# Post-layernorm transformer layer on eight Trainium2 cores: bf16 operands for the layernorm sums, and two barriers replaced by single waits

## What is computed

```python
x = L0_attn_hidden_states                      # (2, 4096, 2048) f32
x = _layernorm(x + _L0_attn_ref(x, Wq, Wk, Wv, Wo), axis=-1)
x = _layernorm(x + _L0_ffn_ref(x, gate_w, gate_scale, up_w, up_scale, down_w, down_scale), axis=-1)

def _layernorm(x, axis=-1, eps=1e-5):
    m = jnp.mean(x, axis=axis, keepdims=True)
    v = jnp.var(x, axis=axis, keepdims=True)
    return (x - m) / jnp.sqrt(v + eps)
```

## Time and profile before

| what | us |
|---|---|
| runs shown: median (lowest to highest of 3) | 2450.72 (2443.09 to 2474.64) |
| the profiled execution's own time | 2434.97 |
| its span, slowest core (core 4) | 2433.4 |
| spans of the eight cores | 2421.8 to 2433.4 |
| mean granted PE clock of the cores | 0.919 to 0.924 |
| PE busy | 2058.5 (85% of the span) |
| DVE, ACT, POOL busy | 470.6, 337.3, 129.0 |

### The profile page before, as it was taken

The page is one execution under the profiler, slowest core; times in us unless marked ns, Lnnn a source line. Parts: engine busy times, 40 slices in busy tenths (PEclk is TensorE's granted clock), DMA queues, the critical chain, the costliest instruction groups (busy, mean ns, idle before and its releaser), DMA issues.

```text
span 2433.4 us, 24054 instructions; the slowest of 8 cores (2421.8 to 2433.4 us)
## 1 busy us (share of the span) xinstructions
PE 2058.5 (85%) x9445; PEld 920.9 (38%) x9624; DVE 470.6 (19%) x800; ACT 337.3 (14%) x606; POOL 129.0 (5%) x248
## 2 busy tenths in 40 slices
PE   0799766666997299999999999999999999999970
PEld 0344344444431044444443444444444443444310
DVE  0111166664111501011010000010100100000015
ACT  0000066654003310101100000011010110000030
POOL 4000000000000000000000000000000000000000
PEclk9999866666998599999999999999999999999985
DMA  9443300000420253434433333344343431333003
GB/s 221 60 75 65 69 1 1 1 1 1 78 44 0 37 102 71 86 69 80 77 69 52 69 67 58 67 78 79 70 86 70 79 60 35 59 63 69 18 0 138
DMA packets 38420, 147.70 MB, mean 61 GB/s; under 512 B 4643, under 2 KB 8869, under 8 KB 33958
## 3 DMA queue, kind: packets, MB, share of 16 engines
q0 software_dynamic: 35136, 127.94, 29.9%
q1 hardware_dynamic: 3174, 18.20, 2.3%
HBM read 265.66 MB, written 8.39 MB: 113 GB/s over the span
## 4 chain that ended last, share of the span: by engine, by line
PE 81%; DVE 7%; issue 4%; another core or an unknown queue 3%; ACT 2%; DMA 1%; DVEq 0%; ACTq 0%; POOL 0%; POOLq 0%
PE psD L769 18%; PE psG L659 18%; PE psU L667 18%; PE psW L451 5%; PE psQ L218 5%; PE psD L765 3%; PE pT L339 3%; PE psS L511 2%; PE psS L485 2%; PE pv L352 2%; DVE S_sb L574 1%; DVE S_sb L579 1%; PE psQ L227 1%; PE psH L725 1%
## 5 line engine op out<-in xcount | busy, mean ns | idle before, releaser
L659 PE MATMUL psG<-ab 128*128 128x512 bf16 x2006 | 450.8, 380 | 50.8 <-DMA ab<-wu_is 46.7
L769 PE MATMUL psD<-ab 128*128 128x512 bf16 x2004 | 448.3, 380 | 4.8 <-issue 3.7
L667 PE MATMUL psU<-ab 128*128 128x512 bf16 x2008 | 450.0, 379 | 2.1
L659 PEld LDWEIGHTS psG<-ab 128*128 128x128 bf16 x2048 | 200.7, 98 | 292.4 <-issue 52.2
L769 PEld LDWEIGHTS psD<-ab 128*128 128x128 bf16 x2048 | 195.5, 98 | 276.4 <-issue 50.8
L667 PEld LDWEIGHTS psU<-ab 128*128 128x128 bf16 x2048 | 200.3, 98 | 241.7
L679 DVE SCALAR_TENSOR_TENSOR ab<-psU,scl_sb,sq_sb 128x512 bf16<-128x512 f32 x128 | 90.2, 747 | 808.9 <-PE psU L667 794.2
L694 ACT ACTIVATE sq_sb<-psG,scl_sb 128x512 f32<-128x512 f32 x128 | 88.0, 687 | 774.3 <-PE psG L659 774.3
L339 PE MATMUL pT<-Dm_sb,ab 128*128 128x128 bf16 x640 | 75.8, 269 | 100.4 <-DVE Dm_sb L380 60.7
L779 DVE SCALAR_TENSOR_TENSOR S_sb<-psD,scl_sb,S_sb 128x1024 f32<-128x1024 f32 x32 | 41.1, 1284 | 479.8 <-PE psD L769 479.8
L218 PE MATMUL psQ<-ab 128*128 128x512 bf16 x501 | 112.0, 383 | 9.1 <-DMA ab<-wq_os 8.3
(11 more groups left out here) (72 smaller groups left out, 962.2 us busy)
## 6 DMA issues: line engine op xcount, KB each, us to landing
ab<-wg_is POOLq DMA_DIRECT2D x64, 512.0 KB, 6.0
ab<-wu_is POOLq DMA_DIRECT2D x64, 512.0 KB, 7.8
ab<-wd_os POOLq DMA_DIRECT2D x32, 1024.0 KB, 8.0
ab<-wq_os POOLq DMA_DIRECT2D x16, 512.0 KB, 5.0
ab<-wo_os POOLq DMA_DIRECT2D x16, 512.0 KB, 5.0
y<-S_sb SPq DMA_DIRECT2D x16, 512.0 KB, 7.2
ab<-x_all POOLq DMA_DIRECT2D x16, 256.0 KB, 44.3
ab<-wv_ks POOLq DMA_DIRECT2D x16, 128.0 KB, 31.3
```

The source lines that it names most:

```text
L659: last = t.matmul(psG[i % 2][:, 512 * tt:512 * tt + 512], abv(wgu_o + 4096 * (i % 2) + 128 * k, 128), abv(y1_o + 1024 * k + 512 * tt, 512) ...
L667: last = t.matmul(psU[i % 2][:, 512 * tt:512 * tt + 512], abv(wgu_o + 4096 * (i % 2) + 2048 + 128 * k, 128), abv(y1_o + 1024 * k + 512 * t ...
L769: last = t.matmul(psD[o % 2][:, 512 * tt:512 * tt + 512], abv(wd_o + 4096 * (o % 2) + 128 * i, 128), abv(h_o + 1024 * i + 512 * tt, 512), ...
```

## The change

Three edits, all in the function that builds the program:

1. The two barriers around attention are gone (they stay only in a debugging branch). In their place stand single waits: PE waits for DVE's last K cast (vv) before the scores, and for DVE and ACT (vv, ss) before the Wo projection. SP's load of the masks waits for the last V matmul (tm) and its own first loads (sq).
2. In `emit_ln` ACT first casts all 16 blocks of S_sb to bf16 into ab (at y1_o in the first layernorm, at h_o in the second). PE sums these with the bf16 ones, oncb_sb; each of its first 16 matmuls waits for its block's cast.
3. The squares are written as bf16 into two 512-wide slots of ab behind that copy, and PE sums them with oncb_sb.

The diff, cut to what is spoken of:

```diff
-            barrier()
+                barrier()
+
+            p1_vv = cnt["vv"]
+            p1_tm = cnt["tm"]
+            vt_last = max(vt_mm)
...
         @block.sync
         def _(sy):
+            sy.wait_ge(sq, p0_sq)
+            sy.wait_ge(tm, vt_last)
             inc(sy.dma_start(abv(mask_o, 8 * 640), masks[:, :]), "sq", 16)
...
             @block.tensor
             def _(t):
+                t.wait_ge(vv, p1_vv)
                 for n in range(NIT + 3):
...
-            barrier()
+                barrier()
+
+            p2_vv = cnt["vv"]
+            p2_ss = cnt["ss"]
...
+                @block.tensor
+                def _(t):
+                    t.wait_ge(vv, p2_vv)
+                    t.wait_ge(ss, p2_ss)
+
...
+                ss0_rc = cnt["ss"]
+                c_rc = [ss0_rc + k + 1 for k in range(KC)]
+
+                @block.scalar
+                def _(s):
+                    for k in range(KC):
+                        got = inc(s.copy(abv(rbf_o + 1024 * k, 1024),
+                                         S_sb[:, 1024 * k:1024 * k + 1024]), "ss")
+                        assert got == c_rc[k]
+
...
-                            last = t.matmul(psS1[:1, 512 * tt:512 * tt + 512], onc_sb[:, :1],
-                                            S_sb[:, 1024 * k + 512 * tt:1024 * k + 512 * tt + 512],
+                            if tt == 0:
+                                t.wait_ge(ss, c_rc[k])
+                            last = t.matmul(psS1[:1, 512 * tt:512 * tt + 512], oncb_sb[:, :1],
+                                            abv(rbf_o + 1024 * k + 512 * tt, 512),
...
-                            s.activation(sq_sb[:, 512 * (j % 2):512 * (j % 2) + 512],
+                            s.activation(abv(rbf_o + 16384 + 512 * (j % 2), 512),
...
-                        got = t.matmul(psS2[:1, 512 * tt:512 * tt + 512], onc_sb[:, :1],
-                                       sq_sb[:, 512 * (j % 2):512 * (j % 2) + 512],
+                        got = t.matmul(psS2[:1, 512 * tt:512 * tt + 512], oncb_sb[:, :1],
+                                       abv(rbf_o + 16384 + 512 * (j % 2), 512),
...
-        emit_ln(write_bf16_to=y1_o)
+        emit_ln(write_bf16_to=y1_o, rbf_o=y1_o)
...
-        ln2_done = emit_ln(write_bf16_to=None)
+        ln2_done = emit_ln(write_bf16_to=None, rbf_o=h_o)
```

More of the change, by code:

```diff
@@ L470, in build_nc, with emit_ln @@
         _ln_id = [0]
-        def emit_ln(write_bf16_to=None):
+        def emit_ln(write_bf16_to=None, rbf_o=None):
             _ln_id[0] += 1
```

## The result

The changed kernel took 2410.15 us (median of 9 runs, 2406.02 to 2416.31), the kernel before 2448.2 us (10 runs). The ratio is 0.9874 with a 95% interval of 0.9852 to 0.9895: 1.3% faster, some 31 us. The forecast was 2420.5 us, with 2402 to 2437 as its range, and 1.2%. The ratio leaves out runs in which the cores of one die had a lower granted clock, the median of before doesn't, so it is not the quotient of the medians. The profiled execution took 2406.02 us around a span of 2404.5; its slowest core is core 2, while in before it was core 4. Worked out from the profiled execution of before (2434.97 us), the forecast was 2404.8.

What follows compares the result with a forecast made beforehand. PE was taken to bound the kernel (81% of the wait chain), with savings only in layernorm statistics and at attention's start. Layernorms 25 plus masks 5.2 made 30.2 us off the 2450.72 us median: 2420.5 us, range 2402 to 2437.

Steps and rivals of the forecast that it cites:

- What bounds: Whole kernel: PE is 81% of the wait chain; savings possible only in the two layernorms' statistics and at attention's start.
- Casts and their table load: Start of each layernorm: 16 ACT casts at 0.95 us pace behind a table load, ending 16.6 us after ACT's release.
- PE's second half: Layernorm, after the last cast: PE's gapless matmuls for the sum's second half take 5.5 us (7.3 lower clock, 3.7 upper).
- The loop: Layernorm squares between ACT and PE: 0.625 us a square at upper clock, 0.75 at lower, 0.71 with a third upper.
- The sum per layernorm: ACT's release to DVE's first statistics step: 47.7 us (51.6 to 41.9) against 60.2; 12.5 gained each, 25 for two.
- The masks: Attention's start: earlier masks' load saves 8.3 us of DVE's wait, delays wq 0 by 3.1, net 5.2 us.
- Barriers: Around attention: replacing barriers by waits gains nothing priced above zero, at most 1.12 us; a loss is excluded.
- (a): Rival, chance 0.17: clock stays up through the layernorm statistics; two layernorms gain 36.6, in all 41.8, 2409 us.
- (b): Rival, chance 0.15: clock stays down in the layernorm statistics; 17.2 + 5.2 = 22.4 us gained, 2428 us.
- (c): Rival, chance 0.08: masks stand fully in wq 0's way before the Q projection, 9.2 us late; 24.1 gained, 2426.6 us.
- (d): Rival, chance 0.07: masks' wait at attention's start stays because something else on DVE or ACT is late; 21.9 gained, 2428.8 us.
- (e): Rival, chance 0.03: square loop loses its overlap, each square costing 1.50 us; slower by 15.6 us, 2466 us.

Runs made afterwards that it cites:

- e6: Changed kernel with four slots for the squares instead of two: 39.0 to 41.7 us per layernorm, whole kernel median 2412.4 us of 4 runs.
- e1: Changed kernel with both barriers and the old place of the masks' load back, so the layernorm part alone: ratio 0.9892 to the kernel before.
- e2: Kernel before, old layernorm, with single waits in place of the barriers and the masks loaded early: ratio 0.9992 (0.998 to 1.0003).
- e9: Changed kernel with casts on DVE, squares 1024 wide in three slots, PE summing blocks as they come, masks loaded after the fourth Q tile: 2354.96 us, ratio 0.9647.
- e3: Kernel before with only the barriers replaced by single waits, the masks' load still going out after DVE's last K cast: ratio 1.0022.
- e10: Kernel before, old layernorm, with barriers replaced by waits and the masks' load issued after the fourth Q tile: ratio 0.9991 (0.9976 to 1.0007).
- e7: Changed kernel with only the squares in bf16, the f32 sum of S kept without casts: 2417.09 us in one run, 52.7 to 55.3 us per layernorm.

## Why the prediction was right

Point by point, by its own steps.

- *What bounds.* The layernorm's statistics and the start of attention were the two places; the Wo projection (115.0 us before, 114.6 after) and the stretch from DVE's first statistics step of the first layernorm to ACT's release in the second (1513.0 and 1513.3, means over cores) did not move. Right.
- *Casts and their table load.* Forecast 16.6 us from the release, measured 16.5 (709.68 to 710.97 + 15.24). A load came ahead of each block of casts and of each block of squares (two loads in each of the two layernorms, 1283 ns each), so the Trainium skill's rule ("ScalarE: Activation LUTs", Table sets: the hidden batching unit) that a copy is in every set did not save one here, and where it has 2.66 us for a switch of set (What ACT_TABLE_LOAD costs), the cast started 1.29 us after the load had. Right.
- *PE's second half.* Forecast 5.5 us (3.7 to 7.3); from 726.36 to 732.23 are 5.87, first at the lower and then at the upper level. Right.
- *The loop.* Forecast 0.625 us a square at the upper level, 0.75 at the lower, a third of upper. Measured 1.25 and 1.45 us a pair, so 0.625 and 0.73, and 0.69 in the mean (732.23 to 754.32 for 32). Right, and e6 shows that the round trip is what sets it: with four slots it is out of the way.
- *The sum per layernorm.* Forecast 47.7 us, measured 47.0 to 48.4 on the eight cores, mean 47.7. Forecast gain of both 25 us, e1 alone 26 (22 to 31).
- *The masks.* This is the term that was mis-sized: "8.3 - 3.1 = 5.2 us". e2, with this part alone, gave 2 us with an interval from -1 to 5, so 5.2 lies just outside it. (The changed kernel against e1 would make it 4 us, 0.9874 against 0.9892, with intervals that overlap.) The 8.3 was read from core 4, the one with the longest wait of all: 9.46 us there, 6.16 to 9.46 over the cores, mean 7.6, so 6.9 us go in the mean. The 3.1 us for the wq load was right for e2's mean (3.1) and too small for the change's own profile (mean 3.8, from 0.6 to 6.8 by core). As the delay "if they all go first" it was not the upper end: core 2 waited 12.82 us, 4.1 more than any core of the profiles without the early masks (8.73 at most, in e9). And of the remaining 3.8 us less arrived at the end. One place where it is lost was found, the stretch at half clock at the first layernorm's start in five cores of e2 (1.0 us in the mean); the rest, about 1 to 1.5 us, is below what these runs can place.
- *Barriers.* "Cost and bring nothing", with "a loss is excluded as only waits go". The first half holds only as long as the masks are loaded early: with their load in its old place, e3, the edit cost 5 us. The reason given was wrong. A wait that goes lets something start earlier, and that something (POOL's wo loads) can stand in the way of what is needed first.
- *The rivals.* (a) a clock that stays up, (b) one that stays down, (c) wq late by 9.2, (d) a mask wait that stays, (e) a loop without overlap: none came. (c) was nearest: core 2 lost 6.8 us before wq, more than the 5.5 that its masks' wait had been worth.

So the time was right because its large term was built from links that each had a row, and the small term, in e2 less than half as large as thought, was a sixth of the whole. That the ratio came out within 0.1% of the forecast is in part luck, since e1 and e2 leave each term open by several us. The median is 10 us below the 2420.5 forecast because that was counted from 2450.72 us, a median 16 us above the profiled execution; counted from the profiled execution (2404.8 against 2406.02 us) it is off by one. The rule of "DMA: Bandwidth & Descriptors" in the Trainium skill (Issuing engines are not separate DMA queues), that all loads interleave on the same engines, agrees with e2, e10 and e3: POOL's load is late by SP's (e2: 3.1 us, e10: waits of 1.3 to 3.7), and SP's by POOL's (e3: 3.1 us). The upper bound that the prediction drew from it, the masks' 3.1 us of engine time, did not hold on core 2.

## What to carry to other kernels

The loop over two buffers between two engines took, for a pair, the sum of both engines' latencies and signals; add the links up before choosing a remedy, since more slots (8 us a layernorm in e6), or an idle third engine together with wider pieces and more slots (28 us in e9), gave more here than the bf16 squares by themselves (6.5 us in e7). A load that is moved away from a wait lands beside another load: look for who needs the DMA engines at the new place, and cut it into pieces that fit the slack. A per-core wait is to be read on all cores before it is put into a sum, since the profiled slowest core may be the one where just this wait was longest, as here.

## What the runs showed of the hardware

- With the barriers gone and the masks' load left in its place, the kernel was slower by 0.2% (e3, 1.0022, 1.001 to 1.0033): two loads of another queue went out 1.4 us ahead of it, and it was waited for 3.1 us longer.
- The delay of wq by the masks was of two kinds in the change's profile: 0.6 to 1.5 us on cores 0, 3, 4 and 7, and 6.0 to 6.8 us on cores 1, 2, 5 and 6. The first group had waited 7.6 to 8.3 us before, the second 5.8 to 6.0. In e2's profile the same subtraction gives 0.4 to 5.8 us, and no such groups. Why was not tried.
- DVE cast 128x1024 from f32 to bf16, from S_sb to ab, at 0.6 us each (e9), ACT at 0.95 (profile after).
- In the changed kernel's loop of squares the granted clock fell from 1.00 to 0.50 at about 738; PE had stood idle 0.35 us in every 1.25 before that (profile after, 732 to 738). It did not come back up to the loop's end at 754.3. With four slots (e6, core 4) it stayed at 1.00 through the loop (725 to 741), with three engines (e9, core 4) through the whole stretch. The four f32 passes of L542 behind the loop took 3.56 us at 0.50 and 1.87 us at 1.00.
